# Expert layers whose shares are spread over the partitions by transfers inside SBUF

## The reference

```
# layer 0: 8 experts, 2 chosen per token
pn, sn = l2norm(x @ Wp.T), l2norm(sim_matrix)
gate_scores = pn @ sn.T / temperature
top_v, top_i = top_k(gate_scores, 2);  comb[token, expert] = softmax(top_v)
h = gelu(x @ W1[e] + b1[e]);  eo = h @ W2[e] + b2[e]
out = sum_e eo[e] * comb[:, e]
# layer 2: 8 experts, 2 chosen
probs = softmax(xn @ Wr + br);  scores, idx = top_k(probs, 2)
full[e] = relu(xn @ W1[e] + b1[e]) @ W2[e] + b2[e];  c[e] = relu(b1[e]) @ W2[e] + b2[e]
out = sum_k scores[k] * (full[idx[k]] - c[idx[k]] + sum_e c[e]);  returns x + out
# layer 3: 16 experts and a shared one, 8 chosen
y = sum_e (silu(x @ w_gate[e].T) * (x @ w_up[e].T)) @ w_down[e].T * combine[:, e]  + shared
```

## Time and profile before

| | us |
|---|---|
| median of three runs | 3777.93 (3775.66 to 3779.57) |
| the profiled execution | 3776.22 |
| its span, first to last instruction | 3774.5 |
| TensorE busy in it | 3656.4 |
| layer 0's experts, first hidden product to last addition | 877.41 to 1003.96 |
| layer 2's experts, the same | 3284.97 to 3428.46 |
| layer 3's experts, first product to last | 3660.24 to 3766.81 |

### The profile page before, as it was taken

The page is one execution under the profiler, slowest core; times in us unless marked ns, Lnnn a source line. Parts: engine busy times, 40 slices in busy tenths (PEclk is TensorE's granted clock), DMA queues, the critical chain, the costliest instruction groups (busy, mean ns, idle before and its releaser), DMA issues.

```text
span 3774.5 us, 83457 instructions
## 1 busy us (share of the span) xinstructions
PE 3656.4 (97%) x32078; PEld 1361.2 (36%) x32082; DVE 1781.0 (47%) x1816; ACT 2546.6 (67%) x2585; POOL 503.9 (13%) x1852
## 2 busy tenths in 40 slices
PE   8999999999999999999999999999999999898999
PEld 4333333334433333333333333343222223344443
DVE  3222222224377777778777877753221211344343
ACT  6999999993455555555555555559999999502321
POOL 2222222220000000000000000013322332100210
PEclk9999999999999999999999999999999999999999
DMA  6323232212111111111111110000000000110000
GB/s 197 103 80 96 83 101 86 98 69 64 63 39 44 35 39 40 39 40 39 40 39 40 39 40 11 1 24 4 4 4 4 4 30 2 48 34 1 0 0 6
DMA packets 99634, 162.93 MB, mean 43 GB/s; under 512 B 22388, under 2 KB 39184, under 8 KB 97776
## 3 DMA queue, kind: packets, MB, share of 16 engines
q1 hardware_dynamic: 99312, 158.16, 13.1%
HBM read 93.24 MB, written 64.88 MB: 42 GB/s over the span
## 4 chain that ended last, share of the span: by engine, by line
PE 79%; ACT 12%; issue 5%; DVE 3%; ACTq 0%; DMA 0%; SPq 0%; POOL 0%; DVEq 0%; POOLq 0%
PE ps L1010 18%; PE ps L1035 18%; PE ps L683 11%; ACT probs L1393 7%; PE ps L615 4%; ACT probs L1404 4%; PE ps L898 3%; PE ps L505 3%; PE ps L511 3%; PE ps L880 2%; PE ps L1220 2%; PE ps L1231 2%; PE ps L1271 2%; PE ps L645 1%; PE ps L1285 1%
## 5 line engine op out<-in xcount | busy, mean ns | idle before, releaser
L1521 ACT ACTIVATE probs<-ps 128x1024 f32<-128x1024 f32 x808 | 828.0, 1025 | 587.4 <-PE ps L1010 575.2
L1404 ACT ACTIVATE probs<-ps 128x1024 f32<-128x1024 f32 x1200 | 1119.3, 1031 | 48.8 <-PE ps L615 33.7
L2411 DVE TENSOR_TENSOR vbuf<-vbuf,probs 128x1024 f32<-128x1024 f32 x784 | 953.1, 1223 | 330.8 <-ACT probs L1521 330.8
L683 PE MATMUL ps<-probs,vst 128*32 128x512 f32 x6400 | 843.6, 598 | 27.5 <-ACT probs L1404 24.4
L2208 DVE COPY qs<-ps 128x512 f32<-128x512 f32 (+1 forms) x208 | 141.7, 681 | 563.8 <-PE ps L511 282.8
L1393 ACT ACTIVATE probs<-ps 128x1536 f32<-128x1536 f32 x268 | 362.1, 1623 | 3.4 <-PE ps L663 1.8
L1695 POOL CAST kst<-kb 128x128 fp32r<-128x128 f32 (+1 forms) x800 | 252.4, 316 | 740.8 <-PE ps L683 592.9
L1010 PE MATMUL ps<-probs,kb 64*64 64x512 f32 x2560 | 332.2, 589 | 0.0
L1035 PE MATMUL ps<-probs,qz 64*64 64x512 f32 x2048 | 266.7, 591 | 1.8 <-DVE kb L2436 1.8
L1035 PE MATMUL ps<-probs,kb 64*64 64x512 f32 x2048 | 265.8, 589 | 0.0
L1707 POOL COPY vst<-vbuf 128x36 f32<-128x36 f32 (+1 forms) x816 | 193.9, 238 | 438.6 <-PE ps L683 432.3
(11 more groups left out here) (442 smaller groups left out, 3588.8 us busy)
## 6 DMA issues: line engine op xcount, KB each, us to landing
kv_scratch<-qs SPq DMA_DIRECT2D x192, 256.0 KB, 2.0
kb<-kv_scratch SPq DMA_DIRECT2D x72, 256.0 KB, 2.9
qz<-kv_scratch SPq DMA_DIRECT2D x56, 256.0 KB, 2.9
kb<-k_scratch SPq DMA_DIRECT2D x12, 816.0 KB, 6.9
vbuf<-in_L_ffn_W SPq DMA_DIRECT2D x32, 256.0 KB, 3.1
klo<-kv_scratch SPq DMA_DIRECT2D x32, 256.0 KB, 2.8
qs<-kv_scratch SPq DMA_DIRECT2D x32, 256.0 KB, 2.9
qz<-q_scratch SPq DMA_DIRECT2D x56, 64.0 KB, 2.1
```

Source lines behind the costliest of these rows:

```text
L683: mm = pe.matmul(ps[band, 6 + half, :], vst[:, r, band], probs[:, r, j * HT:(j + 1) * HT], start=start, stop=stop)
L1404: act.activation(probs[:, r, b * T:(b + 1) * T].rearrange("p (h n) -> p h n", h=2), ps[:, 2 * buf:2 * buf + 2, :], ACT.Exp, scale=HD8 ** - ...
L1521: act.activation(pr1[:, (u + (u == LAST1) + 2 * odd) % 4], ps[:, 2 * b:2 * b + 2, :], ACT.Exp, scale=HD64 ** -0.5)\
L2411: dve.tensor_tensor(sum1[:, odd, h], sum1[:, odd, h], e, ALU.add).then_inc(s["added"], 1)
```

## The change

The spreading products, `pick`, the split into two parts and ScalarE's copies go. VectorE copies the turned shares once as they are to `share_rows`, one partition per expert, 1024 numbers of 4 bytes. SyncE then issues one transfer per expert (`row_spread`) whose source is that one row, named 128 times, and whose destination is a buffer of 128 partitions by 1024: two buffers in layers 0 and 2, four in layer 3. All 32 transfers count on one semaphore, and each waits until the one before it has landed; from the third (the fifth in layer 3) on it also waits until its buffer has been read. VectorE multiplies by this buffer.

Beside it, the order of the work around is changed. In layer 0 the hidden products of expert 0 are computed before and while the gate is evaluated, and the softmax over two values is written with Tanh. In layer 2 the ReLUs of an expert are issued around the weighting of the one before, and the sums of relu(b1) @ W2 go to ScalarE (`scale_rows`) and GpSimd. In the LayerNorms one product with `centre_d` (the identity less 1/128) gives the centred value in PSUM; ScalarE squares it from there, and VectorE copies it afterwards.

```diff
+        share_rows = flat[0:E16, 5 * T:6 * T]
+        spread = [[place[:, u * T:(u + 1) * T].rearrange("p (h n) -> p h n", h=2) for u in range(count)]
+                  for place, count in ((kbf[:, 5 * T:7 * T], 2), (qz[:, 0:2 * T].bitcast(F32), 2), (qz[:, 0:4 * T].bitcast(F32), 4))]
...
 # TensorE, layers 0 and 2
+            def hidden8(m, e, f, bank, evacuated):
+                n = e + E8 * m
+                if f == 0:
+                    pe.wait_ge(s[f"moe_w{e % 2}"], 32 * (n // 2 + 1))
+                pe.wait_ge(s["hid_ready"], evacuated)
...
+            def output8(m, e, h):
+                n = e + E8 * m
+                if h == 0:
+                    pe.wait_ge(s["eo_used"], n + 1)
...
-                def weight8(n, u, h):
-                    pe.wait_ge(s["ccol_ready"], n + 1)
-                    pe.wait_ge(s["cb_copied"], n * 2 + h + 1)
-                    pe.matmul(ps[:, 6, :], pick[0:64, u:u + 1].to_broadcast([64, P]), shares[:, h, :],
-                              start=True, stop=True).then_inc(s["cb_ready"], 1)
...
-            keep_busy(2, 2)
+            hidden8(0, 0, 0, 0, 2)
+            hidden8(0, 0, 1, 2, 2)
...
 # ScalarE, LayerNorm
-                    act.activation(t2[:, h, :], t1[:, h, :], ACT.Square).then_inc(s["ln_sq"], 1)
+                    act.activation(t2[:, h, :], ps[:, h, :], ACT.Square).then_inc(s["ln_sq"], 1)
...
 # VectorE
+            def rows_out(m, experts):
                 dve.wait_ge(s["turned"], 4 + m)
+                dve.tensor_copy(share_rows[0:experts].rearrange("p (h n) -> p h n", h=2), ps[0:experts, 6:8, :]).then_inc(s["w_copied"], 1)
...
+            def weighted8(m, e):
+                n = e + E8 * m
+                dve.wait_ge(s["moe_acc"], n + 1)
+                dve.wait_ge(s["eo_ready"], n + 3)
+                dve.wait_ge(s["spread_in"], 16 * (n + 1))
...
-                    dve.wait_ge(s["cb_ready"], n + 4 * E8)
-                    dve.tensor_tensor(t1, t1, ps[:, 6:8, :], ALU.mult).then_inc(s["hd_ready"], 1)
+                    dve.wait_ge(s["spread_in"], n * 16 + 32 * E8)
+                    dve.tensor_tensor(t1, t1, spread[2][buffer], ALU.mult).then_inc(s["hd_ready"], 1)
...
 # SyncE
+            def row_spread(m, e):
+                if e or m:
+                    sp.wait_ge(s["spread_in"], 16 * (e + E8 * m))
+                sp.dma_start(spread[m][e % len(spread[m])].rearrange("p h n -> p (h n)"), share_rows[e:e + 1, :].unsqueeze(1).to_broadcast([1, P, T]))\
+                    .then_inc(s["spread_in"], 16)
...
+                    if e == 1:
+                        rows_set(m)
+                        row_spread(m, 0)
+                        row_spread(m, 1)
+                    elif e:
+                        sp.wait_ge(s["eo_used"], e + E8 * m)
+                        row_spread(m, e)
...
+            rows_set(2)
+            for e in range(E16):
+                if e >= 4:
+                    sp.wait_ge(s["hd_ready"], e - 2)
+                row_spread(2, e)
```

More of the change, by code:

```diff
@@ L89 @@
 NIDENT = 2
-NCONST = 26
+NCONST = 28
 ADDED = {1: 0, 3: H * ST}
@@ L868, in attention8, with slot8 @@
                 product8(NG - 1, 1).then_inc(s["wo_ready"], 1)
+            def slot8(e):
+                return vbuf[:, e % 2 * 2 * F:(e % 2 + 1) * 2 * F]
+            def hidden8(m, e, f, bank, evacuated):
[3 more added lines that the diff above has]
+                pe.wait_ge(s["hid_ready"], evacuated)
+                for h in range(2):
+                    mm = pe.matmul(ps[:, bank + h, :], slot8(e)[:, f * P:(f + 1) * P], z[:, h, :], start=True, stop=True)
+                mm.then_inc(s["h_ready"], 1)
@@ new lines, in output8 @@
+            def output8(m, e, h):
+                n = e + E8 * m
+                if h == 0:
+                    pe.wait_ge(s["eo_used"], n + 1)
+                for f in range(NF):
+                    pe.wait_ge(s["hid_ready"], n * NF + f + 3)
+                    mm = pe.matmul(ps[:, 4 + h, :], slot8(e)[:, F + f * D:F + (f + 1) * D], hid[:, f, h, :],
+                                   start=(f == 0), stop=(f == NF - 1))
+                if h == 1:
+                    mm.then_inc(s["eo_ready"], 1)
@@ L871, in experts8, with turn_shares @@
+            def turn_shares(m, experts):
+                pe.wait_ge(s["comb_ready"], m + 1)
+                for t in range(NT):
+                    mm = pe.transpose(ps[0:experts, 6 + t // 4, (t % 4) * P:(t % 4 + 1) * P],
+                                      route[:, 7, t * experts:(t + 1) * experts], ident[:, :])
+                mm.then_inc(s["turned"], 1)
             def experts8(m):
-                def expert(i, u):
-                    e = i * 2 + u
+                for e in range(1, E8):
@@ L908, in expert @@
[L908 to L918 removed]
+                        hidden8(m, e, f, 2 * (f % 2), n * NF + f + 1)
@@ L1162, in _ @@
             mm.then_inc(s["g_proj"], 1)
+            for f in range(NF):
+                hidden8(1, 0, f, 2 * (f % 2), E8 * NF + f + 1)
+            for h in range(2):
+                output8(1, 0, h)
+            turn_shares(1, E8)
             experts8(1)
@@ L1272, in hidden16 @@
                 mm.then_inc(s["hg_ready"], 1)
-            def weights16(n, u):
-                pe.wait_ge(s["ccol_ready"], n + 2 * E8)
-                for h in range(2):
-                    mm = pe.matmul(ps[:, 6 + h, :], pick[0:64, u:u + 1].to_broadcast([64, P]), shares[:, h, :],
-                                   start=True, stop=True)
-                mm.then_inc(s["cb_ready"], 1)
             def output16(n, start, stop):
@@ L1577, in _ @@
             load_table(5, ACT.Sqrt)
-            experts8(1)
+            for e in range(E8):
+                scale_rows(e)
             def turned16(n):
@@ L1806, in _ @@
             stage2()
-            weights8(1)
+            for e in range(E8):
+                pool.wait_ge(s["rb_ready"], e + 1)
+                if e == 0:
+                    pool.tensor_copy(scaled_sum, scaled).then_inc(s["rb_summed"], 1)
+                else:
+                    pool.wait_ge(s["rb_summed"], e)
+                    pool.tensor_tensor(scaled_sum, scaled_sum, scaled, ALU.add).then_inc(s["rb_summed"], 1)
             mode3 = mode_of(pool, 3)
@@ new lines, in weighted8 @@
+            def weighted8(m, e):
[3 more added lines that the diff above has]
+                dve.wait_ge(s["spread_in"], 16 * (n + 1))
+                if m == 0:
+                    dve.scalar_tensor_tensor(out=t1, in0=ps[:, 4:6, :], scalar=b2c[:, 0, e:e + 1], in1=spread[m][e % 2],
+                                             op0=ALU.add, op1=ALU.mult).then_inc(s["eo_used"], 1)
+                else:
+                    dve.tensor_tensor(t1, ps[:, 4:6, :], spread[m][e % 2], ALU.mult).then_inc(s["eo_used"], 1)
@@ L2317, in sums_of, with summed8 @@
+            def summed8(m, e):
+                n = e + E8 * m
+                dve.wait_ge(s["eo_used"], n + 2)
+                dve.tensor_tensor(t2, t2, t1, ALU.add).then_inc(s["moe_acc"], 1)
             def sums_of(layer, first, count, mode):
@@ L2679, in _ @@
             dve.tensor_scalar(r16(7), r16(2), ROUTE_SCALE, None, ALU.mult).then_inc(s["comb_ready"], 1)
-            dve.wait_ge(s["turned"], 6)
-            dve.tensor_copy(shares[0:E16], ps[0:E16, 6:8, :]).then_inc(s["w_copied"], 1)
-            dve.wait_ge(s["w_copied"], 6)
-            dve.tensor_tensor(shares[32:32 + E16], ps[0:E16, 6:8, :], shares[0:E16].bitcast(F32), ALU.subtract)\
-                .then_inc(s["w_copied"], 1)
-            with dve.Fori(1, E16 + 1) as n:
-                expert16(n, True)
+            rows_out(2, E16)
+            with dve.Fori(0, E16 // 4) as i:
+                for u in range(4):
+                    expert16(i * 4 + u + 1, u)
             dve.wait_ge(s["y_ready"], E16 + 2)
```

266 lines of the change are left out of this document (111 added, 155 removed).

## The result

| | before | after |
|---|---|---|
| median, us | 3778.06 (4 runs, 3775.66 to 3779.57) | 4118.62 (4 runs, 4117.55 to 4120.25) |
| the profiled execution | 3776.22 | 4117.55 |
| its span | 3774.5 | 4115.8 |

The changed kernel takes 1.0902 times as long (95% interval 1.0884 to 1.0921). The forecast was 4140 us, 3915 to 4800. The median lies 21 us under it, and the likeliest case, slow transfers of some 21 us each, is the one that came.

The account below looks back on a forecast made before the run. TensorE was taken to bound the kernel, with row transfers to set the three expert layers' ends after the change: 69.6 + 46.7 + 249.3 - 2 = 363.6 us on 3776.22 gives 4140 us, range 3915 to 4800.

Parts of the forecast that it names:

- slow transfers: All three expert layers: a row takes 14 to 41.5 us to land, most likely near 21; 3915 to 4800 us; chance 0.79.
- What bounds it now: Whole kernel before the change: TensorE is busy 97% of the span and holds 79% of the chain.
- The landing time S: Each of 32 row transfers of 512 KB from one partition: 21 us from issue to landing, each microsecond worth 32.
- The chain of 32: Row transfers wait for one another, landing plus 0.4 us per issue: +69.6 in layer 0, +46.7 in layer 2, +249.3 in layer 3.
- queue term of layer 0: Layer 0, six gaps between rows: next expert's weights and key loads go ahead in the queue, 1.8 us each, 10.8 us.
- the rest: LayerNorms: 0.3 us each, six or seven of nine on the path, -2 us, bounds 0 and 6.
- What is removed: Spreading products, layer starts and LayerNorm waits: some 52 us gained if transfers cost nothing, giving 3724 us.
- the spreading product: Expert layers: two of 0.43 us per expert in layer 0 (6.0 us); 16 x 0.65 = 10.4 us in layer 3.
- The signs: Profile after: rows landing in about 21 us, DMA releasing VectorE's weighting in all three layers, layer 3 experts every 21.4 us.
- late weights: Layers 0 and 2: weights queue behind a slow row; products start 1 to 3 us after landing, hidden under 21; no chance given.
- The free read: Rival, all expert layers: reading one partition costs nothing extra, landing 2.7 to 5 us, time 3724 to 3730; chance 0.16.
- The hidden middle case: Rival: landing 5 to 14 us hides in layers 0 and 2; layer 3 pays 16 x (S - 4.95); chance 0.03.

Follow-up runs that it names:

- 16 neighbours: Changed kernel with each 512 KB transfer reading partitions 0 to 15, 8 times each, instead of one partition 128 times: 3758.04 us (one run).
- 16 numbers per row: Changed kernel with each transfer carrying 16 of its row's 1024 shares, the rest of the buffer keeping what was there: 3719.05 us, ratio 0.9846.
- LayerNorm alone: Kernel before the change with only the change's LayerNorms (centring by one product, square from PSUM, copy after it): 3774.32 us against 3778.36, ratio 0.9991.
- through DRAM: Changed kernel with the shares stored once per layer to DRAM and each row read 128 times from there: 3724.63 us, again 3726.72, ratio 0.9862 both times.
- half rows: Changed kernel with each transfer carrying half of its row, 256 KB, the second half of the tokens keeping old buffer contents: 3844.58 us (one run).

## Why the prediction was right

**What bounds it now: right.** The transfers took the place of TensorE at the head of the chain in all three expert layers.

**The landing time S: right**, 20.7 against the 21 taken, and this was the whole case, since each microsecond is worth 32. But the way to it was partly luck. It extrapolated one load *into* 32 partitions to one read *out of* 1, over bounds of 2.7 and 180 us, and its two readings gave 17 and 28. (With its own rounded figures the first is 17.5.) The assumption under it, that the side with few partitions sets the rate whether it reads or writes, holds for the reading side (20.7 from one partition, 3.7 from DRAM into the same 128); for the writing side there is still only the load into 32 partitions that it started from. Its form, a constant factor for every quartering, fails: from 16 neighbours to 1, two quarterings, the moving time grows 3.6 times, 1.9 each; but 16 partitions spread out take half as long as 16 neighbours, which no count of partitions tells. The estimate that the prediction worked out from the Trainium skill, SBUF — State Buffer, section Door 1: The DMA port swizzle, S = 20.6 and 4127 us, came nearer, at 8.4 us from the median instead of 21.

**The chain of 32: right, with three terms too large.**
- The issue of 0.4 us between two rows was added to S. It lies within it: the view counts landing from the issue, and rows follow each other at 20.76 us in layer 3, 20.8 in layer 2. Seven, seven and fifteen issues were 2.8, 2.8 and 6 us too much.
- The queue term of layer 0, 6 x 1.8 = 10.8 us for weights and keys ahead of the next row, did not come. Rows land 20.9 us apart in layer 0, where keys are loaded, and 20.8 in layer 2, where they aren't. The weights and keys go beside the row; it is they that wait (6.6 us in the middle to landing instead of 3.1), not the row.
- S was too large by 0.1 to 0.24 us, by the distance of the rows: 5.8 us in all.

| | forecast | measured | the difference |
|---|---|---|---|
| layer 0 | +69.6 | +54.7 | -14.9: queue -10.8, issues -2.8, S -0.6, first issue 0.65 us earlier |
| layer 2 | +46.7 | +43.5 | -3.2: rows -4.1 (issues -2.8, S -1.3), first issue 0.9 us later |
| layer 3 | +249.3 | +241.6 | -7.7: rows -9.8 (issues -6.0, S -3.8), first issue 1.6 us later, last products at the lower clock +0.6 |
| the rest | -2 | +1.5 | +3.5 |

In layer 3 the first issue comes 10.99 us after the first product instead of 9.4. The group of sixteen products L1281 ahead of the transposes takes 8.84 us instead of 7.14, at a granted clock of 0.79, part of it at the lower of the two levels (1.2 and 2.4 GHz), where it was 1.00, the higher one throughout, before. Of the kernel after, timeline and stretch:

```profile
3760.81 8.84 PE L1281 MATMUL ps<-work,kb 128*128 128x512 f32 x16
```

```profile
3761.00:3769.00 8.00, 8.00 (x15) 3.23 (x15) 4.97 (x32) 3.60 (x4) 0.00 (x0) 0.79 0.01 2
```

The kernel with 16 numbers per row has the same 8.84, so it does not come from the slow transfers. TensorE's work ahead of it does not tell the two kernels apart: in the 20 us from 3741 it was busy for 17.2 us, in the same 20 us of the kernel before (from 3640) for 17.0. The cause is open. The rest's 1.5 us were not followed up: executions of one kernel differ by more (3775.66 to 3779.57 before), and up to the gate, ahead of all the rows, the kernels already differ by 1.2 us (its first product starts at 868.85 before, 869.52 after, 868.44 with 16 numbers per row, 869.64 with LayerNorm alone).

**What is removed: the right places, somewhat too little.** By the kernel with 16 numbers per row, layer 0 gains 14.5 us (forecast 11.3), layer 2 29.3 (27.5), layer 3 12.6 (10.9), the rest 1.1 (2); together 57.5 against 52. The term that was mis-sized is the spreading product. I priced it at its own 0.43 us, or at 0.65 up to the next product; but its neighbours in the earlier trace rows take 3.63 us for eight products where 16 take 6.87, so each half has 0.2 us more at the change from one to the other. Without it, an expert of layers 0 and 2 is 32 x 0.429 = 13.73 us, and one of layer 3 12 x 0.429 = 5.15: 0.63 and 0.85 us per spreading step. None of this shows in the kernel after, where the rows set the end, as the prediction said when it did not subtract it.

**The signs: held, but for layer 2.** The prediction had VectorE's weighting released by DMA in all three layers. That came for 7 of 8 rows in layer 0 and 16 of 16 in layer 3, but for 2 of 8 in layer 2, where the late weights hold TensorE instead: it starts at 3421.94, 1.4 us after the issue that follows the landing of a row (3420.57), within the 1 to 3 us that the prediction gave. That this costs nothing beyond the rows at such an S is as it said: they come 20.8 us apart all the same.

**The rivals.** The free read did not come, but its time did, as soon as the source was another: 3724 to 3730 was its price, and through DRAM it is 3724.63 and 3726.72. The hidden middle case had its sign turn at S near 8: by its rule 6.9 us give 3755 and 11.1 us give 3822. The kernel with neighbours took 3758.0 and the one with half rows 3844.6, on removals that were some 5 us larger than reckoned; what the rule lacked is the first row of each layer, which no buffer hides, and the one late set of weights. At its upper end the middle case contradicts itself: by its own rule S = 14 gives 3869, and the 3916 stated is the slow chain's 4140 less 7 x 32. The low end of the range, 3915, rests on that second number; with S at 20.7 it was not put to the test.

## What to carry to other kernels

A transfer that reads one partition many times is priced by that partition: 512 KB took 20.7 us whatever was read in it, and no number of buffers helps when each transfer waits for the one before. (Rows issued without that wait were not run; what an overlap of them would give is open.) Look at both sides of a transfer for how many partitions they touch and how they are spread; the same row from DRAM cost 3.7 us and one trip of 1.8 us, which made the changed kernel 1.4% faster than the one before instead of 9.0% slower. And price a small instruction between large ones by what its neighbours would take without it, not by its own row.

## What the runs showed of the hardware that I had not expected

- An issue on SyncE can take 15 us. L2886 at 910.77 held SyncE for 15.36 us behind a slow row, where such an issue took 0.44; so whatever SyncE has to do next waits as well. With half rows it took up to 6.8 us.
- A row read from one partition keeps the core's DMA engines busy 83% of the time at 25 GB/s. The busy share of DMA alone does not tell the bytes moved: 31% went with 83 GB/s when the source was 8 partitions.
- The landing time followed the spacing of the source partitions: 6.9 us from 16 neighbours, 4.3 to 4.4 from every second or every eighth. From 8 partitions, four apart, rows came 6.23 us apart, with 8 pieces of 4 KB on the way at a time instead of up to 16.
